# Layers 1 and 2 of a four-layer expert kernel: the first two loads of second weights wait for the gathered rows of both first blocks

## What is computed

```python
x = x + L0_ffn(L0_cond(x, ...), ...)   # 8 experts, hidden width 1024
x = x + L1_ffn(L1_cond(x, ...), ...)   # 8 experts, hidden width 1024, the best one per token
x = x + L2_ffn(L2_cond(x, ...), ...)   # 8 experts, hidden width 512, the best one per token
x = x + L3_ffn(L3_cond(x, ...), ...)   # 32 experts of width 128, the best 6, and a shared one
```

```python
logits = x @ Wr + br
idx = jnp.argmax(logits, axis=-1)
gates = take(softmax(logits), idx)
for ei in range(8):
    h = gelu(xf @ W1[ei] + b1[ei])          # first weights
    y = h @ W2[ei] + b2[ei]                 # second weights
    out = out + y * (gf * (idxf == ei))[:, None]
```

## Time and profile before

| What | Value |
|---|---|
| median of 3 runs | 1189.08 us (1188.43 to 1193.44) |
| span of the profiled execution | 1186.7 us |
| TensorE busy | 1033.4 us (87%) |
| VectorE busy | 919.7 us (77%) |
| ScalarE busy | 650.9 us (55%) |
| GpSimd busy | 557.8 us (47%) |
| q1 (SP's loads and stores) | 161.45 MB, 40.4% of 16 engines' span |
| q0 (GpSimd's gathers and scatters) | 44.19 MB, 15.4% of 16 engines' span |
| chain that ended last | PE 72%, DVE 11%, DMA 6%, issue 5%, ACT 3% |

### The profile page before, as it was taken

How to read it: one execution, slowest core, us unless ns; L and a number is a source line. 1 busy time by engine, 2 the same in 40 slices (tenths; PEclk the granted TensorE clock), 3 DMA queues, 4 the chain that set the end, 5 groups by cost and what they waited for, 6 DMA issues and landing times.

```text
span 1186.7 us, 26177 instructions
## 1 busy us (share of the span) xinstructions
PE 1033.4 (87%) x7845; PEld 977.9 (82%) x7845; DVE 919.7 (77%) x1572; ACT 650.9 (55%) x1407; POOL 557.8 (47%) x375
## 2 busy tenths in 40 slices
PE   6249999999999999999968749999859948889896
PEld 5139999999999999999966649998759946778785
DVE  7877888888888888888847768785748854866795
ACT  4228676767676767676624547672457625223221
POOL 1313788878887888788740033542046620000000
PEclk9569999999999999999986869999879979889998
DMA  7355877777778777868632167653367753030202
GB/s 211 123 170 202 247 218 238 230 253 210 246 225 254 209 246 225 256 205 253 171 46 68 54 239 258 232 185 89 114 222 238 233 162 110 14 89 24 94 14 72
DMA packets 85095, 206.25 MB, mean 174 GB/s; under 512 B 16738, under 2 KB 58482, under 8 KB 71218
## 3 DMA queue, kind: packets, MB, share of 16 engines
q1 hardware_dynamic: 60530, 161.45, 40.4%
q0 software_dynamic: 24512, 44.19, 15.4%
HBM read 170.85 MB, written 34.75 MB: 173 GB/s over the span
## 4 chain that ended last, share of the span: by engine, by line
PE 72%; DVE 11%; DMA 6%; issue 5%; ACT 3%; SPq 0%; DVEq 0%; POOL 0%; POOLq 0%; ACTq 0%
PE ps L812 23%; PE ps L813 22%; PE ps L814 22%; PE ps L909 2%; DMA y_rows<-w_raw,slot_rows 1%; PE ps L824 1%; DVE hidden_lo L1657 1%; DMA scratch<-in_L_w 1%; DVE x_tok L1980 1%; DVE featB_lo L1657 1%; DMA z_tok<-in_L_w 1%; DVE featA_lo L1657 1%; DMA x_rows<-w_raw,slot_rows 1%; DMA z_tok<-y_rows 1%; DMA w_raw<-z_rows,slot_rows 1%
## 5 line engine op out<-in xcount | busy, mean ns | idle before, releaser
L1423 ACT ACTIVATE hidden_f<-ps,b_block 128x256 f32<-128x256 f32 x480 | 247.2, 515 | 189.4 <-PE ps L814 179.9
L703 POOL DMA_INDIRECT x_tok<-z_gate_rows,slot_rows x88 | 239.8, 2725 | 122.3 <-DVE block_gates L1938 68.2
L1424 ACT ACTIVATE hidden_hi<-ps,b_block 128x256 fp32r<-128x256 f32 x480 | 249.4, 520 | 0.0
L812 PE MATMUL ps<-w_hi,featA_hi 128*128 128x256 f32 (+2 forms) x724 | 208.1, 287 | 8.7 <-DVE scratch L2329 5.4
L813 PE MATMUL ps<-w_lo,featA_hi 128*128 128x256 f32 (+2 forms) x724 | 207.2, 286 | 0.0
L814 PE MATMUL ps<-w_hi,featA_lo 128*128 128x256 f32 (+2 forms) x724 | 207.2, 286 | 0.0
L812 PE MATMUL ps<-featB_hi,hidden_hi 128*128 128x256 f32 x712 | 203.0, 285 | 3.8 <-DVE hidden_lo L1657 3.8
L813 PE MATMUL ps<-featB_lo,hidden_hi 128*128 128x256 f32 x712 | 199.7, 280 | 0.0
L814 PE MATMUL ps<-featB_hi,hidden_lo 128*128 128x256 f32 x712 | 199.0, 279 | 0.0
L1657 DVE TENSOR_TENSOR hidden_lo<-hidden_f,hidden_hi 128x512 fp32r<-128x512 f32 x276 | 178.0, 692 | 18.5 <-ACT hidden_hi L1424 16.0
L731 POOL DMA_INDIRECT x_rows<-w_raw,slot_rows x88 | 145.4, 1653 | 40.3 <-issue 29.0
(11 more groups left out here) (477 smaller groups left out, 2548.8 us busy)
## 6 DMA issues: line engine op xcount, KB each, us to landing
scratch<-in_L_w SPq DMA_DIRECT2D x54, 1024.0 KB
z_tok<-in_L_w SPq DMA_DIRECT2D x32, 1024.0 KB
x_tok<-in_L_w SPq DMA_DIRECT2D x22, 1024.0 KB
b_block<-in_L_ffn_b POOLq DMA_DIRECT2D x66, 128.0 KB
z_tok<-y_rows SPq DMA_DIRECT2D x12, 512.0 KB, 5.4
z_tok<-in_L_w SPq DMA_DIRECT2D x12, 512.0 KB
scratch<-in_L_w SPq DMA_DIRECT2D x12, 512.0 KB
z_rows<-z_tok SPq DMA_DIRECT2D x8, 512.0 KB, 2.9
```

What stands on the lines that cost most here:

```text
L703: gp.indirect_dma_start(XBL[L][:, k, tt, :], None, ZD if L else ZD0, bass.IndirectOffsetOnAxis(ap=TOK[:, q * BTT + tt:q * BTT + tt + 1], a ...
L812: nc.tensor.matmul(out, lh, rh, start=first, stop=False)
L1423: act.activation(HF[:, f // 2, part], ps, func, bias=b1)
L1424: act.activation(HTh[:, k, f // 2, part], ps, func, bias=b1).then_inc(s_hhi[L], 1)
```

## The change

One wait of SP becomes two, in the branch for layers 1 and 2. The second weights of blocks (0, 0) and (0, 1) are loaded only when the gathered rows of both first blocks have landed, and no longer when those of block (0, 0) have. Nothing else differs: the instructions of the other engines and their order are the same, and SP's transfers keep their order.

```diff
                     sp.wait_ge(s_gate, L + 1)
-                    sp.wait_ge(s_xb[L][0], 16 * BTT)
+                    for k in range(2):
+                        sp.wait_ge(s_xb[L][k], 16 * BTT)
                     for k in range(2):
                         load_w2(0, k, first[k])
                 with sp.Fori(0, STEPS[L]) as i:
```

## The result

Over 20 runs each, the changed kernel takes 1193.21 us in the median and the kernel before 1188.62 us, 4.6 us less. The ratio on record, which comes with a 95% interval and which I go by, is 1.0034 (1.0022 to 1.0046), so the change costs about 4.0 us (0.0034 x 1188.62; by the interval 2.6 to 5.5 us). That is under the 0.5% that the prediction took as its bound. The interval excludes that nothing changed; how far one such comparison can be trusted is taken up at the end of the experiments. Two of the eight executions of the copy of the kernel before, which took 1738 and 5126 us, are left out of its ratio there.

What follows compares the result with a forecast made beforehand. TensorE was taken to set the pace in layer 1, by how far its start at 723.88 us moves. Layer 1's +1.5 and +1.3 and layer 2's +0.6 make +3.4 on 1189.08: 1192.5 us, range 1187.4 to 1196.0.

Steps and rivals of the forecast that it cites:

- sum for layer 1: Layer 1: +1.5 us for the start of TensorE's next product and +1.3 us for lower clock, together +2.8 us.
- the clock: Layer 1: TensorE's idle grows from 1.35 to 4.8 us and lowers its clock; +1.3 us, bounds 0 and 1.7.
- the wait that goes: Layer 1: TensorE's 1.50 us idle for block (0, 1)'s rows, held behind the weight loads, before its second transposes disappears.
- The release of SP: Layer 1: SP held until 701.6 instead of 697.11 us, 4.5 us later, with rows landing 1.8 us after GpSimd is through.
- The landing of the third load: Layer 1: first weights of block (1, 0) land at 713.3 instead of 710.4 us, with 1.09 MB to be made up.
- What it does to TensorE: Layer 1: ScalarE starts 1.95 us later, so TensorE's next product starts at 725.4 instead of 723.88 us: +1.5, bounds -1.5 to +3.1.
- Layer 2: Layer 2: SP held 1.2 us longer, ScalarE's load wait about 1.5 instead of 0.92 us; +0.6 us, bounds 0 and 1.2.
- the gain that stands: Layer 1: the load lands by 709.85 us, the 1.5 us is gained whole, layer 2 unchanged: 1187.6 us; chance 0.12.
- The level case: Layer 1: the load lands at about ScalarE's old start, 711.35 us; layer 2 +0.2: about 1189.5 us; chance 0.25.
- the second rival: Both layers: the loads' delay reaches TensorE whole, +7.4 us in sum: 1196.5 us; chance 0.10.
- The delay that goes through whole: Layer 1 +3.1 us and 1.7 of clock, layer 2 SP held 2.6 us: +7.4, 1196.5 us; chance 0.10.
- That nothing happens: Block (0, 1)'s rows land no earlier than SP's old issue plus little, so nothing changes; chance 0.03.

Runs made afterwards that it cites:

- the kernel whose clock held: Changed kernel plus 46 transposes that nobody reads, filling TensorE's idle in layer 1; ratio 0.9996 against the kernel before.
- 32 and 46 products: Changed kernel plus 32 or 46 unread transposes on TensorE in layer 1, behind block (0, 0)'s first product; ratios 1.0012 and 0.9996 against the kernel before.

## Why the prediction held

The forecast was 1192.5 us, +3.4; measured was +4.0 (+4.6 by the medians), and +2.7 by the mean of the profiles' distances in layer 1. In layer 1 its mechanism is what the rows show, step by step. That its sum for layer 1, +2.8, lies so near to +2.7 is in part luck: the late load and the clock cost as much as its terms or more (1.5 to 2.3 and 1.7 to 2.0 us, for 1.5 and 1.3), and the wait that goes was worth more than its 1.5 us, so the misses offset each other.

- **The wait that goes.** TensorE's second transposes wait for nothing in all nine profiles in which layer 1 has the new wait. The loads were what held the rows: SP, which waits for the last of them, is released 4.4 to 6.4 us after the first transposes, and with the old wait TensorE has them only after 9.0 to 9.4 us. The gain was taken from one profile, 1.50 us; the other three with the old wait show 1.82 to 2.29 us, and these idles brought the lower clock along, which the 1.50 us did not. The copy's distance is 1.5 us longer for it. The difference isn't in the rows. At the first transposes the granted clock is at 1.2 GHz in all profiles; in the profile before it rose only 7.4 us later, in the other three after 5.9 to 6.1 us (in the copy it is on average 0.63 in the window from 706 us, 5.2 to 6.2 us after them), so that TensorE came to its second transposes 7.79 us after the first, and in the others 7.14 to 7.22 us. The wait removed is thus worth more than the prediction gave it. The window of the profile before in which the clock rose:
```profile
704.00:705.00 1.00, 0.81 (x5) 0.60 (x4) 0.08 (x1) 0.79 (x3) 0.00 (x0) 0.80 1.17 283
```
- **The release of SP.** Predicted 4.58 us after the first transposes (701.6 - 697.02); measured 6.42 us in the profile after, 5.19 in its copy and 4.60 with the wait in layer 1 only. The 1.8 us from GpSimd to the landing is the lower end of what came.
- **The landing of the third load.** Predicted 11.7 us after the release (713.3 - 701.6); measured 10.9 (713.93 - 703.07), 11.5 and 11.9 us. The count of 1.09 MB to be made up, and the rate from the earlier trace rows, gave the right landing. Together with the release, the load landed 17.28, 16.65 and 16.49 us after the first transposes, where 16.28 was predicted. ScalarE's timelines, copy of changed and wait in layer 1 only:
```profile
715.84 1.91 ACT L1402 ACTIVATE featB_hi<-z_tok 128x2048 fp32r<-128x2048 f32 x1 [4.65 <-DMA z_tok<-in_L_w]
```
```profile
715.19 1.91 ACT L1402 ACTIVATE featB_hi<-z_tok 128x2048 fp32r<-128x2048 f32 x1 [4.46 <-DMA z_tok<-in_L_w]
```
- **What it does to TensorE.** Predicted +1.5 us with the clock left out; the kernel whose clock held shows +2.26 us, and the three profiles of the change, less their clock, +1.5 to +2.3 us (31.20 - 2.02, 30.21 - 1.66 and 30.16 - 1.77, each less 26.86). The mechanism is right and the term up to 0.8 us too small, because ScalarE's start moved by 2.2 to 3.0 us (14.33 against 16.49 to 17.28 us after the first transposes) and not by 1.95. Of the bounds, -1.5 to +3.1, the upper one was the nearer, as taken.
- **The clock.** Predicted +1.3 us from an idle of 4.8 us; the idle was 5.73 to 5.93 us, and the cost 1.7 to 2.0 us. The bound of 1.7 us was too low: it came from a fall that lasted 3.4 us, and here the clock stayed down for 6.8 us.
- **Layer 2.** Predicted: SP 1.2 us later, ScalarE's wait 1.5 us, +0.6 us. The profile after shows SP 1.4 us later and no growth of the wait. One profile is too few here, as ScalarE's wait goes from 0.90 to 2.79 us in the five with both the new wait and the old load order in this layer (changed, its copy, wait in layer 2 only, 32 and 46 products; the bias loads in place). Their mean is 1.59 us; the three with the old wait and order have 0.74 to 1.22 us, in the mean 0.96. TensorE's way from the first transposes to the product of (1, 0) goes from 16.97 to 17.50 us in the mean, but the single values overlap (16.45 to 17.53 and 17.17 to 18.12 us). Over the whole layer the five take 83.9 us in the mean, and the three 84.4. So ScalarE's longer wait is there in the mean, and the +0.6 us isn't shown: over the whole layer the means go the other way, and the time of layer 2 alone, 0.9993, can neither show nor exclude it.

Of the rivals, the gain that stands fell with ScalarE's wait of 4.67 us. The level case asked for a landing at ScalarE's old start; it landed 2.2 to 3.0 us later (14.33 against 16.49 to 17.28 us after the first transposes). In the other two profiles with the old wait and order ScalarE started at 15.77 and 15.79 us, so this case was nearer than one profile let it seem. (Its -0.4 us, 723.4 against 723.88, should read -0.5, and the upper end of the range, 1196.0, lies a little under the second rival's 1196.5; neither matters to the forecast.) The delay that goes through whole was near in layer 1 in the profile after (+4.34 us against 4.8), and failed in layer 2, where it asked for 2.6 us. That nothing happens fell with TensorE's wait before its second transposes, which is gone.

The Trainium skill's advice to issue a DMA early and wait late ("DMA: Bandwidth & Descriptors", section "Rules for kernel authors") is borne out here for one load of three. The first weights of (1, 0) cost 1.5 to 2.3 us and the clock when they come late; the second weights of both blocks can wait for the rows, and TensorE's wait before its second transposes goes when they do. No run shows a cost of their later issue as long as no other load is put ahead of both.

## What to carry to other kernels

When a wait is added on an issuing queue, follow every transfer behind it to its first reader: here the two loads that the wait was put before had cover, and the third in line, which the diff doesn't mention, paid. Before giving such a wait up, try the order of what stands behind it; by the distances, one place in the queue was worth as much as the whole loss. And where an effect is a few tenths of a per cent, compare the same stage in several profiles of each kernel, from the same event to the same event, rather than spans.

## What the runs showed of the hardware

- **Idles and the clock.** Idles of TensorE of 1.03 us (46 products) and of 1.35 and 1.50 us left the granted clock at 2.4 GHz. In layer 1, those of 1.82, 2.02, 2.08, 2.18, 2.26, 2.27 and 2.29 us each brought 3.4 us at 1.2 GHz, and those of 5.5 to 5.9 us before the product of block (0, 1) 6.8 us, the end of the idle included. The prediction had put the cost of a longer idle under that of the one of 1.96 us. The length alone doesn't decide, though. In layer 2, before the product of block (1, 0), idles of 1.79 us (wait in layer 1 only), 2.65 us (copy of changed) and 3.82 us (wait in layer 2 only) brought the 3.4 us, and those of 2.22 us (copy of before) and 2.81 us (46 products) left the clock high. What decides, no run here shows. TensorE's timeline and one window for the idle of 2.81 us:
```profile
889.66 0.38 PE L813 MATMUL ps<-w_hi,featB_hi 128*128 128x256 f32 x1 [2.81 <-DVE w_lo L1661]
```
```profile
890.00:950.00 60.00, 58.54 (x492) 58.14 (x491) 52.10 (x75) 43.80 (x103) 43.10 (x42) 1.00 0.79 244
```
- **Gathers beside loads.** With the loads running, the rows of a gather took 6.6 us to be usable, and in the earlier trace rows 15 packets of q0 stand beside 205 of q1. The Trainium skill, "DMA: Bandwidth & Descriptors", section "Queues, rings and completion order", says that each engine takes turns between the queues that have work, packet by packet. These packets aren't shared out evenly, and the measurement decides for the time; whether the gather's packets were not yet there to be moved, no run here shows. With q1 empty, the landing still took 1.8 to 3.7 us.
